# The histogram of the sources is summed in the sort's main loop instead of the setup

## The reference, cut to what matters

```python
src, dst = ...                       # 200000 edges, 12500 nodes
ones_e = jnp.ones(src.shape[0])
out_deg = jnp.clip(jax.ops.segment_sum(ones_e, src, num_segments=N), 1.0)
feat_n = feat * jax.lax.rsqrt(out_deg)[:, None]
...
in_deg = jnp.clip(jax.ops.segment_sum(ones_e, dst, num_segments=N), 1.0)
rst = rst * jax.lax.rsqrt(in_deg)[:, None]
# layer 0 also needs, for each edge, w = silu(silu(s @ W1 + b1) @ W2 + b2) @ W3 + b3
```

## Time and profile before

| what | value |
|---|---|
| median of the runs | 18225.36 us |
| the profiled execution's own time | 18361.17 us |
| its span | 18359.4 us |
| mean granted TensorE clock, of full speed | 0.663 |
| TensorE, VectorE, ScalarE, GpSimd busy | 60%, 56%, 24%, 49% |
| HBM | 141 GB/s over the span |

### The profile page before, as it was taken

How to read it: one execution, slowest core, us unless ns; L and a number is a source line. 1 busy time by engine, 2 the same in 40 slices (tenths; PEclk the granted TensorE clock), 3 DMA queues, 4 the chain that set the end, 5 groups by cost and what they waited for, 6 DMA issues and landing times. The chain is left out here.

```text
span 18359.4 us, 330326 instructions
## 1 busy us (share of the span) xinstructions
PE 11073.9 (60%) x72558; PEld 8512.2 (46%) x72559; DVE 10232.6 (56%) x36116; ACT 4433.1 (24%) x11901; POOL 9038.2 (49%) x10038
## 2 busy tenths in 40 slices
PE   6555555555553666566497466674456775557886
PEld 5333333333332555555386344442235664336776
DVE  9555555555552233333486477675256555776776
ACT  0111111111110222222211133102520113556665
POOL 0466666566563455555676344554530445553332
PEclk9767667776775666666555555776566655557888
DMA  9522222222223222222432499875674777784544
GB/s 376 224 62 66 65 65 63 63 64 65 63 66 72 51 58 57 58 58 57 72 68 48 83 305 301 256 239 169 204 227 128 241 241 237 261 261 166 174 170 142
DMA packets 2144353, 2590.03 MB, mean 141 GB/s; under 512 B 892241, under 2 KB 1761818, under 8 KB 2144194
## 3 DMA queue, kind: packets, MB, share of 16 engines
q1 hardware_dynamic: 1749158, 1741.66, 32.4%
q0 software_dynamic: 353792, 655.17, 11.2%
q10 hardware_dynamic: 41244, 191.56, 2.7%
HBM read 1738.44 MB, written 848.86 MB: 141 GB/s over the span
## 5 line engine op out<-in xcount | busy, mean ns | idle before, releaser
L566 POOL DMA_INDIRECT edges_by_dst<-rec,pos x1568 | 1540.2, 982 | 1993.8 <-DVE rec L501 1541.4
L989 POOL DMA_INDIRECT sc_rows<-src_table,sc_idx x1664 | 1581.7, 951 | 1457.6 <-DVE sc_tp L1087 806.2
L566 POOL DMA_INDIRECT edges_by_cell<-rec,pos x1568 | 1551.0, 989 | 528.4 <-issue 527.8
L1759 PE MATMUL ex_rows<-table,ex_oh 128*128 x6528 | 1142.0, 348 | 1015.3 <-DVE ex_stage L1735 312.0
L1039 PE MATMUL sc_loc<-dst_table,sc_ohT 128*128 x3328 | 770.9, 404 | 1123.4 <-ACT sc_ohT L1005 1074.5
L1759 PEld LDWEIGHTS ex_rows<-table,ex_oh 128*128 128x128 bf16 x6528 | 770.6, 133 | 1386.4 <-issue 1344.6
L2258 PE MATMUL at_part<-cell_edge_term,key_in_block 128*66 128x128 f32 x8704 | 1218.8, 304 | 255.6 <-issue 214.4
L2258 PEld LDWEIGHTS at_part<-cell_edge_term,key_in_block 128*66 128x66 f32 x8704 | 1133.2, 158 | 325.0 <-issue 312.8
L1098 DVE TENSOR_TENSOR sc_qk<-sc_loc,sc_kv 128x256 f32<-128x256 f32 x416 | 176.6, 424 | 1970.1 <-ACT sc_kv L1018 1392.0
L530 DVE SCALAR_TENSOR_TENSOR junk<-rowb,keycol,earlier 128x128 f32<-128x128 f32 (+1 forms) x3136 | 1151.6, 414 | 201.8 <-issue 197.8
L1039 PEld LDWEIGHTS sc_loc<-dst_table,sc_ohT 128*128 128x128 f32 x3328 | 664.1, 297 | 1262.5 <-issue 1262.4
(11 more groups left out here) (402 smaller groups left out, 26457.5 us busy)
## 6 DMA issues: line engine op xcount, KB each, us to landing
ex_keys<-src_key_rows SPq DMA_DIRECT2D x1632, 128.0 KB
gs_rows<-dst_rows_by_src SPq DMA_DIRECT2D x1088, 192.0 KB
rowb<-sort_key_rows SPq DMA_DIRECT2D x392, 512.0 KB
ex_keys<-dst_key_rows SPq DMA_DIRECT2D x1088, 128.0 KB
dst_rows_by_src<-patY ACTq DMA_DIRECT2D x1, 104448.0 KB
rows_by_src<-ex_stage SPq DMA_DIRECT2D x544, 192.0 KB
scored_dst_rows_by_src<-patZ ACTq DMA_DIRECT2D x1, 71808.0 KB
scored_rows_by_src<-ex_stage SPq DMA_DIRECT2D x544, 132.0 KB
```

The source lines that it names most:

```text
L566: nc.gpsimd.indirect_dma_start(out=out, out_offset=bass.IndirectOffsetOnAxis(ap=pos[:, u, k, j:j + 1], axis=0), in_=row, in_offset=None).t ...
L989: nc.gpsimd.indirect_dma_start(out=rows[:, u, j, :], out_offset=None, in_=tabS, in_offset=bass.IndirectOffsetOnAxis(ap=idx[:, u, j:j + 1], ...
L1759: m = nc.tensor.matmul(rows[k][u % deep][r // 2][:, r % 2, 0:W], oh[k][:, u % deep, r * P:(r + 1) * P], t3[:, bass.ds(held[k][u], 1), :].r ...
```

## The change

The comparison of the sources' low parts and the matmul for the sources go out of the histogram loop. The sort's loop now makes eight parts instead of six (two more behind c = 3), and adds the group's eight columns of the sources into `srcps`, a bank that stays open over the whole loop, behind fc2 at c = 2. At that place TensorE waits until all eight parts of its group are made; at the group's start it waits for six. Behind the loop the source histogram is masked, turned and copied.

```diff
-    parts = ((0, HI, 0), (0, HI, 1), (0, LO, 0), (1, HI, 0), (0, LO, 1), (1, HI, 1))
-    HALF0 = 4
+    parts = ((0, HI, 0), (0, HI, 1), (0, LO, 0), (1, HI, 0), (0, LO, 1), (1, HI, 1), (1, LO, 0), (1, LO, 1))
+    HALF0, LOOKED_UP = 4, 6
...
                             nc.vector.tensor_tensor(
-                                onehot[:, u, LO, :, :, :], bcast(K.iota4[:, :, 0:2], 1, [P, 2 * PAIRS, P, 2]),
-                                bcast(keys(LO), 2, [P, 2 * PAIRS, P, 2]), ALU.is_equal).then_inc(s_oh, 1)
+                                onehot[:, u, LO, 0:PAIRS, :, :], bcast(K.iota4[:, :, 0:2], 1, [P, PAIRS, P, 2]),
+                                bcast(keys(LO, 1), 2, [P, PAIRS, P, 2]), ALU.is_equal).then_inc(s_oh, 1)
...
-                                nc.tensor.matmul(hps[0][0:NB, :, :], tile_onehot(onehot, u, HI, 0, j)[:, 0:NB], lo_and_cell(onehot, u, j),
-                                                 start=False, stop=False)
-                                m = nc.tensor.matmul(hps[1][0:NB, 0, :], tile_onehot(onehot, u, HI, 1, j)[:, 0:NB], tile_onehot(onehot, u, LO, 1, j),
+                                m = nc.tensor.matmul(hps[0:NB, :, :], tile_onehot(onehot, u, HI, 0, j)[:, 0:NB], lo_and_cell(onehot, u, j),
                                                      start=False, stop=False)
...
-                    for k, src, q in ((0, hps[0][:, 0, :], 0), (1, hps[0][:, 1, :], 1), (2, hps[1][:, 0, :], 0)):
-                        step(dve, nc.vector.tensor_tensor(hist[:, k, :], src, notph[:, q, :], ALU.mult))
+                    for k in range(2):
+                        step(dve, nc.vector.tensor_tensor(hist[:, k, :], hps[:, k, :], notph[:, k, :], ALU.mult))
...
-                    step(dve, nc.vector.tensor_copy(K.deg[:, :, :], dps[:, :, 0:NB]))
+                    step(dve, nc.vector.tensor_copy(K.deg[:, 0, :], dps[:, 0:NB]))
...
                 weights(NG, NG % 2)
+                dve.wait_ge(s_srch, 1)
+                nc.vector.tensor_tensor(hist[:, 2, :], srcps[:, :], notph[:, 0, :], ALU.mult).then_inc(s_srcm, 1)
+                dve.wait_ge(s_srct, 1)
+                nc.vector.tensor_copy(K.deg[:, 1, :], look[0][:, 0, 0, 0:NB])
...
                         pe.wait_ge(s_oc, g + 1)
-                        pe.wait_ge(s_one, (g + 1) * NK)
+                        pe.wait_ge(s_one, g * NK + LOOKED_UP)
...
                                 nc.tensor.matmul(xps[u][:, :], w2d[:, :], h1[:, :], start=True, stop=True).then_inc(s_m2, 1)
+                                pe.wait_ge(s_one, (g + 1) * NK)
+                                for j in range(SG):
+                                    nc.tensor.matmul(srcps[:, :], tile_onehot(onehot, u, HI, 1, j), tile_onehot(onehot, u, LO, 1, j),
+                                                     start=False, stop=False)
...
+                nc.tensor.matmul(srcps[:, :], K.zero[:, :], K.zero[:, :], start=False, stop=True).then_inc(s_srch, 1)
+                pe.wait_ge(s_srcm, 1)
+                pe.wait_ge(s_pick, NG * PAIRS + LOOKS)
+                nc.tensor.transpose(look[0][:, 0, 0, :], hist[:, 2, :], K.ident[:, :]).then_inc(s_srct, 1)
```

More of the change, by code:

```diff
@@ L267, in sort_edges @@
         with ExitStack() as pctx:
-            hps = [pctx.enter_context(nc.psum_tensor(f"hps{k}", [P, 2, P], F32)) for k in range(2)]
+            hps = pctx.enter_context(nc.psum_tensor("hps", [P, 2, P], F32))
             tps = pctx.enter_context(nc.psum_tensor("tps", [P, 3], F32))
             bps = pctx.enter_context(nc.psum_tensor("bps", [P, 512], F32))
-            dps = pctx.enter_context(nc.psum_tensor("dps", [P, 2, P], F32))
+            dps = pctx.enter_context(nc.psum_tensor("dps", [P, P], F32))
             nps = pctx.enter_context(nc.psum_tensor("nps", [P, P], F32))
@@ L312, in _, with keys @@
                             dve.wait_ge(s_h, g + 1)
-                            def keys(half):
-                                return hilo[:, bass.ds(g, 1), half, :, :].rearrange("p o k (q t) -> p (o k q) t", t=2)
+                            def keys(half, ends):
+                                return hilo[:, bass.ds(g, 1), half, 0:ends, :].rearrange("p o k (q t) -> p (o k q) t", t=2)
                             nc.vector.tensor_tensor(
                                 onehot[:, u, HI, :, 0:NB, :], bcast(K.iota4[:, 0:NB, 0:2], 1, [P, 2 * PAIRS, NB, 2]),
-                                bcast(keys(HI), 2, [P, 2 * PAIRS, NB, 2]), ALU.is_equal)
+                                bcast(keys(HI, 2), 2, [P, 2 * PAIRS, NB, 2]), ALU.is_equal)
                             nc.vector.tensor_tensor(
-                                onehot[:, u, LO, :, :, :], bcast(K.iota4[:, :, 0:2], 1, [P, 2 * PAIRS, P, 2]),
-                                bcast(keys(LO), 2, [P, 2 * PAIRS, P, 2]), ALU.is_equal).then_inc(s_oh, 1)
+                                onehot[:, u, LO, 0:PAIRS, :, :], bcast(K.iota4[:, :, 0:2], 1, [P, PAIRS, P, 2]),
+                                bcast(keys(LO, 1), 2, [P, PAIRS, P, 2]), ALU.is_equal).then_inc(s_oh, 1)
                 @block.tensor
@@ L329, in _ @@
                         nc.tensor.transpose(kps[n % 2][0:w, :], keyf[:, 1 - n // len(kchunks), c:c + w], K.ident[:, :]).then_inc(s_kt, 1)
-                    nc.tensor.matmul(hps[0][:, :, :], zero[:, :], bcast(zero[:, :], 1, [P, 2, P]), start=True, stop=False)
-                    nc.tensor.matmul(hps[1][:, 0, :], zero[:, :], zero[:, :], start=True, stop=False)
+                    nc.tensor.matmul(hps[:, :, :], zero[:, :], bcast(zero[:, :], 1, [P, 2, P]), start=True, stop=False)
                     with pe.Fori(0, NG // 2) as i:
@@ L410, in _ @@
                     nc.tensor.matmul(tps[:, :], triU[:, :], rows[:, :], start=True, stop=True).then_inc(s_tp, 1)
-                    for k in range(2):
-                        m = nc.tensor.transpose(dps[:, k, :], hist[:, 2 * k, :], K.ident[:, :])
-                    m.then_inc(s_dp, 1)
+                    nc.tensor.transpose(dps[:, :], hist[:, 0, :], K.ident[:, :]).then_inc(s_dp, 1)
                     pe.wait_ge(s_nc, 2)
@@ L614, in _ @@
                 nc.tensor.matmul(xps[1][:, :], K.zero[:, :], bcast(K.zero[:, :], 1, [P, 4, P]), start=True, stop=True).then_inc(s_m3, 1)
+                nc.tensor.matmul(srcps[:, :], K.zero[:, :], K.zero[:, :], start=True, stop=False)
                 pe.sem_inc(s_pick, LOOKS)
```

5 lines of the change are left out of this document (3 added, 2 removed).

## The result

| kernel | median | runs | ratio to before, 95% interval |
|---|---|---|---|
| before | 18226.21 us | 6 | 1 |
| after | 18313.62 us | 6 | 1.0044 [1.0032, 1.0056] |

The change costs 0.44%, 87 us between the medians; 18300 was forecast. The profiled execution after took 18317.95 us, near its median. That of before lay 135 us above its own, in stages behind the sort that the change doesn't touch, so the two are compared up to the sort's end only.

What follows compares the result with a forecast made beforehand. VectorE was taken to bound the setup's histogram loop, GpSimd's scatter batches and its wait for L501 the sort's loop. Minus 18.6 plus 95 gives plus 76 us on 18225.36: 18300 forecast, range 18185 to 18450.

Steps and rivals of the forecast that it cites:

- The setup, minus 18.6: Histogram loop ends 104 us earlier, but ScalarE's fill issue holds the block: 18.1 us gained, plus 0.5 us of smaller work.
- Rival (B): Setup gives all its 104 us, because the fill's queue doesn't hold the block or shrinks: 18216 or 18121; chance 0.06.
- The loop, plus 95: Sort's loop: 0.6 us for each of 140 ordinary groups, 84 us, and 0.4 us for 28 others, 11 us.
- VectorE's c = 3 pick comes up to 0.85 us later for TensorE, then 0.7 to 0.84 us for its own two: Sort's loop, last pair: added matmuls, then the two added comparisons, make the next group start some 1.5 us later.
- rival (A): Sort's loop hides all added work under GpSimd's 20.4 us batch of scatters; only the setup's gain remains: 18207; chance 0.25.
- The delay eats smooth time: Sort's loop: delay at a batch's smooth start pushes more of the next group's first two pairs into or behind the crawl.
- the crawl: Sort's loop: other engines slow until GpSimd's scatter batch ends, VectorE's instructions starting 0.7 us apart.
- the long wait: Sort's loop: GpSimd's wait of about 17.5 us, once in seven groups; 0.4 us added to each of 28, 11 us.
- The ordinary waits: Sort's loop: GpSimd's waits of 3.1 to 6.0 us in five of seven groups, mean 3.9; 0.6 us added to each.
- (C): All added work in the sort's loop is exposed, 367 us less the setup's gain: 18574; chance 0.10.
- (D): Sort's loop: each added comparison blocks a GpSimd scatter for its 0.42 us, 165 us in all: 18372; chance 0.07.
- (E): Sort's loop: the repeating seven-group pattern of GpSimd's waits breaks, saving 10 us each seven groups, 280 in all: 18021; chance 0.07.

Runs made afterwards that it cites:

- e1: Changed kernel with neither the two added comparisons nor the eight added matmuls in the sort's loop, only the changed setup: ratio 0.9991 to the kernel before.
- e8: Changed kernel with the two large fills issued in pieces by SP in the sort's loop, not by ScalarE's queue in the setup: 1.0003 of before.
- e9: Changed kernel with both the fills in the sort's loop and the eight matmuls ahead of the wait for h1: 18147.73 us, 0.9935 of before.
- e3: Changed kernel with the two added comparisons a group but without the eight matmuls: ratio 0.9983 to the kernel before.
- e11: Changed kernel without the comparisons, its eight matmuls replaced by two of 128x512 with zeros at the same place: 0.9992 of before.
- e5: Changed kernel without the comparisons, each of its eight matmuls cut to 8 by 8 columns: 1.0014 of before.
- e6: Changed kernel without the comparisons, with sixteen matmuls a group instead of eight: 1.0092 of before.
- e4: Changed kernel with the eight matmuls ahead of TensorE's wait for h1 instead of behind fc2, nothing left out: 1.0003 of before.

## Why the prediction was right, and where it was not

**The setup, minus 18.6: right.** Forecast: the loop ends near 359, 85 us are lost, `hist` starts at 446. Measured: 358.7, 86.67 and 445.40; the first batch starts 19.4 us earlier. e1 puts it at 16 us. Rival (B) is out, and e8 and e9 show why: take the queue's instruction away and `hist` starts 86 us earlier. The comparison of 1024 elements came to 690 ns, where 0.52 ns an element from the earlier trace rows gave 677.

**The loop, plus 95: the size nearly, the working not.** The profiles give 0.66 us a group, 130 us in all; the medians give 87 + 19 = 106. The forecast made 1.5 us of delay from 0.84 us of comparisons and 0.7 to 0.84 us of matmuls, and let 0.6 of it through. Two steps of that failed.

- "VectorE's c = 3 pick comes up to 0.85 us later for TensorE, then 0.7 to 0.84 us for its own two". The second half costs nothing: e3 has all of the comparisons and is not slower than e1. For this part the cover that rival (A) described was real. As a whole (A) is false; e1 against after is 0.0053.
- "The delay eats smooth time". The forecast had the next group arrive later in the batch, so that more of it falls into the crawl. It doesn't arrive later: the copy's input is ready 6.8 us into the batch before and 6.5 after. What grows is how long ScalarE and VectorE stand still with their inputs there, 4.8 to 9.5 us ahead of the copy and 3.6 to 7.2 us of VectorE's idling in a group, and the record behind VectorE carries this to the next batch. Nor is the measure a time: e11 takes the same 0.73 us and costs nothing, e5 takes 0.30 and costs. The term should have been read from the number of instructions behind fc2, eight matmuls with eight weight loads, where TensorE goes from 50 matmuls a group (9794 in 196 groups) to 58. The prediction named this as what would make it wrong, "a crawl that depends on how many instructions TensorE and VectorE run": for TensorE's it is so, for VectorE's (e3) not.

That the sum came out within 14 us of the median is therefore partly luck: 0.6 us was chosen for five of seven groups and 0.4 for the long wait, by an argument in which half of the delay was free and the other half was priced by the wrong measure. The ordinary waits that it was sized from were also those of one stretch: 3.9 us in the mean of the earlier trace rows, 4.45 over the loop.

**The price grows faster than the number.** Sixteen instead of eight cost 0.0101 instead of 0.0032 over e1; two, as wide ones, cost 0.0001. A term linear in the number would have missed this.

**The other rivals.** (C) would have been 18574. (D): a scatter's issue takes 0.980 us in the mean after and 0.986 before, and e3 has the comparisons and is not slower. The rule of the Trainium skill (SBUF — State Buffer, Who interferes with whom), that a VectorE instruction with two SBUF inputs contends with a GpSimd instruction that reads SBUF, has no sign here: 392 more comparisons leave the issue at 981 ns. Whether such an issue reads SBUF at all, no run shows. (E): the pattern of sevens stays after (26 starts without a wait, 26 long ones, against 26 and 25). It can shift, as e1's 41 pairs show, but e1's ratio says that this gains nothing that is seen.

**What stays open.** Why the number and the place of small TensorE instructions decide how long ScalarE and VectorE stand still while GpSimd issues. A supply of instructions that runs dry while GpSimd issues would fit the crawl, in which VectorE's instructions start 0.7 us apart, and the stops; but no run measured such a supply, and the traces show no transfer of instructions from memory between 600 and 5400 us in before, after and e1 to e6, so at least that way of running dry is out. Nor is it settled why the comparisons, free by themselves, add 0.0021 on top of the matmuls.

## What to carry to other kernels

Work that is added at the place where an engine has just been let go, and on which others wait, is to be counted in instructions as well as in time; try the same work one wait earlier, where the engine would stand idle anyway: here that was worth 0.4%. When a loop in a block is shortened, look for the longest queue instruction of the same block first, since it becomes the block's end; moving that transfer into a later stage with idle DMA engines gave 75 us of the 93 by the ratios (after to e8), and 124 with the eight matmuls at the better place (e4 to e9). And an engine that starts late beside a wait isn't yet its cause: ask whether the waiting instruction needs it.

## What the runs showed of the hardware

- Two bf16 matmuls of 128x512 take as long as eight of 128x128 (0.73 and 0.72 us from the first to the next line's), and eight of 128x8 still take 0.30 us. By the cost to the loop, two wide ones are free and eight narrow ones are not.
- The issue of a large fill holds its queue for long while the DMA engines are full: 385.06 us for patZ. It isn't held to the transfer's end: the queue is free at 444.69 us, and the engines are still full at 640. Cut into pieces of one group each and issued from SP's loop, an issue takes 0.37 us (e8).
- ScalarE can stand for 15 us with its input ready while GpSimd issues scatters, and start when they end (2731.72 against 2716.9 above), and VectorE for 8.77 us; the idle time is shown as "remote", which looks like a wait for another engine. With eight small matmuls a group more behind fc2, VectorE does so for 7.2 us of a group instead of 3.6.
